# The quantised feed-forward of a two-layer decoder as one unrolled stream in place of four loops

## What is computed

```python
def act_qdq(x):
    qmax = 2.0 ** (ACT_BITS - 1) - 1.0
    scale = jnp.maximum(jnp.max(jnp.abs(x)) / qmax, 1e-12)
    return jnp.clip(jnp.round(x / scale), -qmax - 1.0, qmax) * scale

x = act_qdq(x)
up = act_qdq(x @ lpbq_dequant(w_up).T)
gate = act_qdq(x @ lpbq_dequant(w_gate).T)
sig = fixed_qdq_u16(jax.nn.sigmoid(gate))
gate = act_qdq(gate * sig)
o = act_qdq(gate * up)
return o @ lpbq_dequant(w_down).T
```

## Time and profile before

| | |
|---|---|
| three runs, us | 1874.87, 1876.58, 1877.08 |
| the profiled execution, us | 1876.91 |
| its span, first to last instruction, us | 1875.3 |
| mean granted clock of TensorE | 0.92 of full |
| busy: TensorE / DVE / ACT / POOL | 83% / 53% / 46% / 23% of the span |
| DMA traffic | 107 MB, 57 GB/s over the span |

### The profile page before, as it was taken

The page is one execution under the profiler, slowest core; times in us unless marked ns, Lnnn a source line. Parts: engine busy times, 40 slices in busy tenths (PEclk is TensorE's granted clock), DMA queues, the critical chain, the costliest instruction groups (busy, mean ns, idle before and its releaser), DMA issues. The chain is left out here.

```text
span 1875.3 us, 27409 instructions
## 1 busy us (share of the span) xinstructions
PE 1555.1 (83%) x10044; PEld 1078.4 (58%) x10044; DVE 986.9 (53%) x2215; ACT 871.9 (46%) x1820; POOL 435.4 (23%) x563
## 2 busy tenths in 40 slices
PE   4999999999875499999959999999996699740189
PEld 2666766676653287877736666666665343310177
DVE  3565657766655252222135565656453336888822
ACT  2346565555453122121126565556663337877611
POOL 3123233434333200000056444543331000000000
PEclk9999999999987699999979999999997799875599
DMA  3340111101311434343431111110000000000112
GB/s 103 125 150 19 42 32 45 39 30 42 105 35 49 144 104 149 109 144 120 116 107 42 31 43 33 50 38 1 16 15 23 0 0 1 0 0 0 46 66 68
DMA packets 99630, 107.08 MB, mean 57 GB/s; under 512 B 25266, under 2 KB 88508, under 8 KB 99504
## 3 DMA queue, kind: packets, MB, share of 16 engines
q1 hardware_dynamic: 93360, 88.83, 15.2%
q0 software_dynamic: 6144, 16.57, 2.7%
HBM read 63.59 MB, written 42.01 MB: 56 GB/s over the span
## 5 line engine op out<-in xcount | busy, mean ns | idle before, releaser
L1866 ACT ACTIVATE c_pr<-bank,c_nmax 128x256 f32<-128x256 f32 x256 | 118.1, 475 | 151.0 <-DVE c_nmax L1947 150.9
L2417 PE MATMUL bank<-wdT,hT_all 128*128 128x256 f32 x384 | 89.1, 397 | 119.5 <-DVE hT_all L2395 119.5
L1619 POOL TENSOR_SCALAR c_pr<-c_pr,c_rsum 128x256 f32<-128x256 f32 x256 | 128.7, 518 | 223.1 <-DVE c_rsum L1952 223.0
L1386 ACT ACTIVATE b_G<-bank 128x320 f32<-128x320 f32 x128 | 56.0, 437 | 209.5 <-PE bank L1336 209.5
L1336 PE MATMUL bank<-b_XT,shared 128*128 128x320 f32 x512 | 153.3, 434 | 0.0
L2417 PEld LDWEIGHTS bank<-wdT,hT_all 128*128 128x128 f32 x384 | 76.8, 201 | 132.2 <-DVE hT_all L2395 120.7
L1350 PE MATMUL bank<-shared,b_G 128*128 128x256 f32 x640 | 142.2, 379 | 0.0
L1350 PEld LDWEIGHTS bank<-shared,b_G 128*128 128x128 f32 x640 | 120.9, 190 | 17.8
L947 DVE TENSOR_TENSOR a_A<-bank,a_causal 128x512 f32<-128x512 f32 x128 | 79.4, 683 | 73.8 <-PE bank L475 73.7
L1947 DVE TENSOR_REDUCE c_nmax<-bank 128x2 f32<-128x512 f32 x128 | 82.2, 683 | 55.0 <-PE bank L1658 54.9
L1336 PEld LDWEIGHTS bank<-b_XT,shared 128*128 128x128 f32 x512 | 91.7, 191 | 27.0 <-issue 0.2
(11 more groups left out here) (287 smaller groups left out, 3403.5 us busy)
## 6 DMA issues: line engine op xcount, KB each, us to landing
shared<-L_ffn_w SPq DMA_DIRECT2D x32, 512.0 KB, 6.0
t_slots_in<-a_h SPq DMA_DIRECT2D x20, 512.0 KB, 6.7
shared<-t_slots_in SPq DMA_DIRECT2D x15, 640.0 KB, 6.9
t_slots_out<-b_Y SPq DMA_DIRECT2D x15, 640.0 KB, 4.1
a_xin<-x SPq DMA_DIRECT2D x8, 512.0 KB, 3.7
a_xr<-x SPq DMA_DIRECT2D x8, 512.0 KB, 3.7
t_x_a<-hT_all SPq DMA_DIRECT2D x8, 512.0 KB, 2.9
shared<-t_x_a SPq DMA_DIRECT2D x8, 512.0 KB, 4.1
```

Of the source, the lines that this page charges most:

```text
L1386: a.activation(G[e % 2][:, f, HC * m:HC * m + HC], P[2 + n % 2][:, 0:HC], ACT.Gelu).then_inc(q.g_ready, 1)
L1619: p.tensor_scalar(pr[k][:, e, u, :], pr[k][:, e, u, :], rsum[k][:, e, u:u + 1], 1.0, ALU.mult, ALU.mult).then_inc(q.pr_ready, 1)
L1866: a.activation(pr[t % 2][:, e, u, :], P[e][:, S * u:S * u + S], ACT.Exp, bias=nmax[t % 2][:, e, u:u + 1], accum_out=sums[t % 2][:, e, u:u ...
L2417: t = p.matmul(P[n % 8][:, 0:D], tl[f"of{k % 2}"][:, f, 128 * j:128 * j + 128], wdT[:, f, :], start=(f == 0), stop=(f == FC - 1))
```

## The change

The feed-forward becomes one block with one set of semaphores: no loop, no block end or clear between its stages.

- At the end of layer 1 POOL runs one `partition_all_reduce` on a scratch column, whose result is not used.
- Input: DVE alone quantises, a group (2 x 512 elements) at a time: groups 0 and 1 ahead of the gate, the others between the gate's magnitudes.
- Gate: 48 units in one run; TensorE goes on with the up units as soon as a bank is free.
- Activation: tiles are now two units (2 x 512 = 1024 elements in each partition), 24 of them. The multiplied activation is written over the gate in `raw` and kept. There is one sigmoid tile (`sig`), two for its uint16 values and three for the gate's int16; every third tile is rounded by ACT, the others by DVE.
- Up values: 13 tiles have room of their own (`up`); 7 go into columns of `hT_all` whose products are done; 4 tiles (8 units) stay in the 8 PSUM banks until they are converted. Units 46 and 47 take the banks of units 42 and 43.
- Product: ACT converts the up value and the kept activation to int16; DVE multiplies and takes the magnitude.
- Down: the rows of x are fetched once the first 8 up tiles are converted, into their room; 8 groups in one run with two int16 tiles; the last group is stored in four parts of 128 KB.

```diff
+                p.partition_all_reduce(rstd[0][:, 0:1], minus[:, 0:1], 128, RMAX).then_inc(q.c_pool, 1)
...
-        make_scales(("x", c.amax, None, None))
-        quantise_input()
...
-            with nc.Fori(0, NG // K) as i:
...
+        IN_BANKS = (19, 20, 22, 23)
+        def unit_bank(m):
+            return P[m % 8] if m < NU - 2 else P[m % 8 - 4]
+        def up_tile(n):
+            if n < NOWN:
+                return pair(up[:, W * n:W * n + W])
+            i = n - NOWN if n < 19 else NG - 2
+            return hT[:, :, T * i:T * i + T]
+        def sig_by_scalar(n):
+            return n % 3 == 2
...
+            @block.sync
+            def _(s):
+                s.wait_ge(q.ui_ready, NG * NT * D // W)
+                for g in range(NG):
+                    s.dma_start(xin[g], x_rows[g]).then_inc(arrived[g], 16)
...
+            @block.tensor
...
+                for m in range(NU):
+                    if m % FC == 0:
+                        p.wait_ge(q.xq_ready, m // FC + 1)
+                    if m >= 8:
+                        p.wait_ge(q.bank_free, m - 7)
+                    product(wgT, m, P[m % 8])
+                for m in range(NU):
+                    p.wait_ge(q.bank_free, NU + m - (7 if m < NU - 2 else 3))
+                    product(wuT, m, unit_bank(m))
...
+            @block.scalar
...
+                def gate_int(n):
+                    if n >= 3:
+                        a.wait_ge(q.act_ready, n - 2)
+                    a.activation(pair(gi[n % 3]), tile(n), ACT.Copy, scale=inv["g"][:, :]).then_inc(q.gi_ready, 1)
+                def sigmoid(n):
+                    if n:
+                        wait_sig_int(a, n - 1)
+                    a.wait_ge(q.gi_ready, n + 1)
+                    a.activation(sig, gi[n % 3], ACT.Sigmoid, scale=scale["g"][:, :]).then_inc(q.sig_ready, 1)
+                def sigmoid_int(n):
+                    a.wait_ge(q.sig_ready, n + 1)
+                    a.wait_ge(q.act_ready, n - 1)
+                    a.activation(sq[n % 2], sig, ACT.Copy, scale=65536.0).then_inc(q.sq_ready_s, 1)
...
+                for m in range(4):
+                    keep_up(m)
+                a.wait_ge(q.scaled, 2)
+                gate_int(0)
+                gate_int(1)
+                sigmoid(0)
+                for n in range(1, NTILE):
+                    if n + 1 < NTILE:
+                        keep_up(2 * n + 2)
+                    sigmoid(n)
+                    if n + 1 < NTILE:
+                        gate_int(n + 1)
+                    if sig_by_scalar(n):
+                        sigmoid_int(n)
+                    if n + 1 < NTILE:
+                        keep_up(2 * n + 3)
+                a.wait_ge(q.scaled, 3)
+                for n in range(NTILE):
+                    if n >= NI:
+                        a.wait_ge(q.prod_ready, n - NI + 1)
...
+                        x = a.activation(pair(u_room[n % NI]), up_tile(n), ACT.Copy, scale=inv["u"][:, :])
+                    x.then_inc(q.ui_ready, 1)
+                    if n:
+                        if n == 1:
+                            a.wait_ge(q.scaled, 4)
+                        a.activation(pair(a_room[n % NI]), tile(n), ACT.Copy, scale=inv["a"][:, :]).then_inc(q.ai_ready, 1)
...
+            @block.vector
...
+                make_scale("x", 0)
+                quantise_input(0)
+                quantise_input(1)
+                for m in range(NU):
+                    gate_magnitude(m)
+                    if m % FC == 1 and m // FC + 2 < NG:
+                        quantise_input(m // FC + 2)
+                v.wait_ge(q.bank_free, NU)
+                largest("g")
+                make_scale("g", 1)
+                for m in range(4):
+                    up_magnitude(m)
+                sigmoid_int(0)
+                for n in range(NTILE):
+                    if n + 1 < NTILE and not sig_by_scalar(n + 1):
+                        sigmoid_int(n + 1)
+                    activate(n)
+                    if n + 2 < NTILE:
+                        up_magnitude(2 * n + 4)
+                    if n + 1 < NTILE:
+                        act_magnitude(n)
+                    if n + 2 < NTILE:
+                        up_magnitude(2 * n + 5)
...
+                largest("u")
+                act_magnitude(NTILE - 1)
...
+                make_scale("u", 2)
+                make_scale("a", 3, (scale["g"][:, :], 1.0 / 65536.0))
+                v.tensor_scalar(pair(a_room[0]), tile(0), inv["a"][:, :], None, ALU.mult).then_inc(q.ai_first, 1)
+                for n in range(NTILE):
+                    product(n)
+                    if n:
+                        product_magnitude(n - 1)
+                product_magnitude(NTILE - 1)
```

More of the change, by code:

```diff
@@ L2107, in feed_forward @@
         P = c.banks
-        ident = c.ident[:, :]
         NTOK = B * S
-        wuT, wgT, wdT = c.wuT, c.wgT, c.wdT
+        NU = NG * FC
+        NTILE = NU // 2
+        W = 2 * T
+        wuT, wgT, wdT, hT = c.wuT, c.wgT, c.wdT, c.hT_all
         raw = sb("raw", [128, FC, NTOK])
[L2112 to L2117, removed]
@@ L2118, in feed_forward @@
-        scale = {k: sb("scale_" + k, [128, 1]) for k in "xugao"}
-        inv = {k: sb("inv_" + k, [128, 1]) for k in "xugao"}
-        unit = {k: sb("unit_" + k, [128, 1]) for k in "ao"}
[L2123 to L2147, removed]
-                            if unit is not None:
-                                step(v.tensor_scalar(gmx[n][:, :], gmx[n][:, :], unit[:, :], None, ALU.mult))
-                            step(v.tensor_scalar(scale[k][:, :], gmx[n][:, :], 1.0 / QMAX, 1e-12, ALU.mult, ALU.max))
-                            step(v.reciprocal(inv[k][:, :], scale[k][:, :]))
-                            if unit is not None:
-                                step(v.tensor_scalar(inv[k][:, :], inv[k][:, :], unit[:, :], None, ALU.mult))
-                        for m in zeroed:
-                            v.memset(m[:, :], 0.0)
-                clear(nc, q)
@@ L2158, in quantise_input @@
-        def quantise_input():
-            with ExitStack() as once:
-                q = signals(nc, once, "xi_ready xq_ready")
-                xi = raw[:, 0:1, :].bitcast(I16)
-                with nc.Block() as block:
-                    @block.scalar
-                    def _(a):
-                        part = xi[:, 0, 0:NTOK]
-                        a.activation(part, c.hT_all[:, 0, :], ACT.Copy, scale=inv["x"][:, :]).then_inc(q.xi_ready, 1)
-                        a.wait_ge(q.xi_ready, 1)
-                        a.activation(c.hT_all[:, 0, :], part, ACT.Copy, scale=scale["x"][:, :])
-                    @block.vector
-                    def _(v):
-                        part = xi[:, 0, NTOK:2 * NTOK]
-                        v.tensor_scalar(part, c.hT_all[:, 1, :], inv["x"][:, :], None, ALU.mult).then_inc(q.xq_ready, 1)
-                        v.wait_ge(q.xq_ready, 1)
-                        v.tensor_scalar(c.hT_all[:, 1, :], part, scale["x"][:, :], None, ALU.mult)
-                clear(nc, q)
@@ new lines, in unit_bank, with tile, kept_until @@
+        def unit_bank(m):
[5 more added lines that the diff above has]
+            return hT[:, :, T * i:T * i + T]
+        def tile(n):
+            f = n % (FC // 2)
+            g = n // (FC // 2)
+            return raw[:, 2 * f:2 * f + 2, T * g:T * g + T]
+        def kept_until(m):
+            return NU + sum(k // 2 not in IN_BANKS for k in range(m + 1))
@@ L2423 @@
+        clear(nc, q)
 class Common:
```

373 lines of the change are left out of this document (169 added, 204 removed).

## The result

| | before | after |
|---|---|---|
| median, us | 1876.83 (4 runs: 1874.87 to 1883.19) | 1807.47 (4 runs: 1804.15 to 1812.24) |
| ratio, 95% interval | | 0.9627 [0.9595, 0.9659] |
| profiled execution / its span, us | 1876.91 / 1875.3 | 1812.24 / 1810.5 |
| a second series on another chip, median, us | 1876.28 (9 runs) | 1804.69 (5 runs), ratio 0.9613 [0.9592, 0.9635] |

The change saves 69 to 72 us of a forecast 77.6. The profiled execution is the slowest of the nine of the changed kernel, so positions in it are told from a mark inside the layers that both kernels share: R, the start of POOL's last reciprocal root of layer 1, at 1444.98 before and 1456.92 after. From R to the span's end it was 430.3 us before and 353.6 after, 76.7 less. The rest of the miss lies ahead of R, in code that is the same.

The account below looks back on a forecast made before the run. Bounds: TensorE in gate and down, DVE in product, three engines almost level in up. Stage ends added in sequence to span 1797.6, time 1799.2, 1799 at the median, 77.6 us (4.1%) less; range 1789 to 1825.

Parts of the forecast that it names:

- The layer's end: Layer 1's end: early reduction takes the 6.8 us first-use gap; input maximum there at 1454.8, not 1458.6.
- the early reduction does nothing: Layer end: first-use cost can't begin before other work is done; real reduction 5.4 us later, 1804; chance 0.12.
- Input by groups: Input quantisation: TensorE starts at 1457.1, not 1468.17; the other seven groups, 1.3 us each on DVE, cost nothing.
- Gate: Gate stage: 48 units without a loop turn, 44.08 us with cold start plus 41.2; TensorE ends at 1542.4.
- Head of the up stage: From gate scale at 1545.2 through copies, gate integers, one table load and sigmoids to the first activation at 1557.0.
- The swap rival: Up stage: Copy and Sigmoid swap tables at each tile, 57 us more, 1856; chance 0.04.
- Activation and up: Up stage after the first activation: DVE bounds closely, 87.8 us, 3.65 a tile; last magnitude at 1645.0.
- hand-offs cost full durations: Two DVE-bound stages: each wait breaks the 0.09 us overlap, 153 operations, 14 us, 1813; chance 0.16.
- TensorE cools: Up stage: waiting drops TensorE to the lower clock, 77 us more, 1876, no gain; chance 0.03.
- The slower rival: Up stage: the single sigmoid tile serialises ACT and DVE, 83 us more, 1882; chance 0.03.
- Product: Product stage: DVE's 24 multiplies and 24 magnitudes take 54.2 us, ACT hidden at 2.12 against 2.26 a tile.
- Down: Down stage: one cold start in place of two, 86.2 us, 1707.4 to 1793.6; last store put at 3.6.

Follow-up runs that it names:

- experiment with the whole input: Changed kernel with all eight input groups quantised on DVE before the first gate unit; first gate matmul 26.18 us after R, +10.17.
- a pass put back: Changed kernel with DVE instead of ACT converting the kept activation to int16 in the product stage; 1824.15 us, a to o reductions 71.90 for 57.06.
- the kernel with loads at the layer's start: Changed kernel with the early reduction moved from the end to the start of layer 1's POOL stream; 1830.47 us, R at 1473.61.
- the kernel before with one turn per loop: Kernel before with each of its four loops run as one turn of twice the length; 1841.42 us for 1879.31.

## Why the forecast was near, and where it failed

- **The layer's end: the step that failed.** "It is a cost of the first use. Moved to 1446.0 it ends at 1452.8" took one idle stretch for one cost. There were two, a 5.3 us drain of POOL under the other engines' last work and a 5.7 us load after it, and moving the load only put the drain behind it. In the clock of before the maximum was due at 1454.8 and came at 1458.97, 4.2 late. That is the outcome of the rival "the early reduction does nothing", which had 0.12 and was priced at 5.4. Its mechanism was not that of the trace: the load did start early. A row of non-busy instructions of POOL would have told it in advance; the view of busy instructions cannot.
- **Input by groups** held: 2.4 us from the reduction to the first gate matmul, for 9.9 before, and the other six groups for nothing (experiment with the whole input: +10.17 when they stand ahead).
- **Gate**: 84.3 us for 85.3. The one cold start cost 1.9 us (84.3 less 48 units of 1.716), not the 2.9 of the earlier trace rows's first turn. It varies: from first matmul to the g reduction the eleven executions of this stage fall into 86.0 to 86.3 and 87.1 to 87.4.
- **Head of the up stage**: first activation at 1560.0 in the clock of before, for 1557.0; 2.6 of the 3.0 were already there at the gate's scale. The one table load was there (1.28 us, and 1.32 from the end of the gate integer to the sigmoid's start), and no second one. The swap rival (0.04) is out.
- **Activation and up**: 89.4 us for 88.0 (87.8 and the largest's 0.2). Of the 1.4 us, 1.1 is a slip of the sum: it counts 23 magnitudes of the activation up to the last one, and the program has 24 (x24 in the row below). The pitch of instructions in a row held, so "hand-offs cost full durations" (0.16) is out: it asked for up to 9.5 us more here. "TensorE cools" (0.03) is out, at 0.94 of clock; it did cool before the last two units (5.60 us for their eight matmuls), hidden as forecast. The slower rival, one sigmoid tile that serialises ACT and DVE (0.03), is out: ACT waited for conversions 11.4 us in all, but DVE waited for sigmoids only in the head (3.8 and 1.2 us) and from the first activation on not at all, busy 99.9% of the time. The groups that show it:

```profile
L2258 ACT ACTIVATE wgT<-d_gate_int,d_scale_g 128x1024 f32<-128x1024 int16 x24 | 27.5, 1148 | 11.4 <-DVE wgT L2355 6.2 <-DVE d_sig_int L2355 5.2
...
L2364 DVE TENSOR_REDUCE d_cur_a<-d_raw 128x1 f32<-128x1024 f32 x24 | 29.1, 1213 | 0.0
```
```profile
1646.72 5.60 PE L2217 MATMUL bank<-hT_all,wuT 128*128 128x512 f32 x8 [7.87 <-DVE d_cur_u L2349]
```

- **Scales**: 1.6 us for 2.4 (u and a) and 1.6 for 2.2 (o). **Product**: 54.6 for 54.2. ACT's 2.12 us a tile stayed under DVE's 2.26. The count of the passes that are left was right, and a pass put back measured +14.8.
- **Down**: 84.6 us for 86.2, one cold start again cheaper than counted; the last store's end 2.7 us after the last addition for 3.6 (a 128 KB part lands 1.7 us after its issue, at the median).
- So behind R the sum was 352.6 and came out 353.6. Lost were 3.9 us up to the first gate matmul and some 2.3 in the head of the up stage, the stage and the product; won back were 1.0 in the gate, 1.6 in the scales, 1.6 in down and 0.9 in the last store. That it came so near is in part luck of signs.
- **Ahead of R: the other step that failed, one not written down.** The sum took the layers in front for fixed. In twelve executions of kernels with the same code there, R lies between 1444.98 and 1459.73 us: 14.7 us apart (the kernel with loads at the layer's start left out). Two executions of the changed kernel itself have 1456.92 and 1446.5, 10.4 us apart, which is nearly all of 1810.5 to 1800.1 in their spans. One place where it arises, in the windows of the three (before, after, after again):

```profile
434.00:436.00 2.00, 2.00 (x3) 0.35 (x2) 0.45 (x2) 0.00 (x0) 1.40 (x2) 0.55 0.27 98
436.00:438.00 2.00, 1.11 (x25) 0.76 (x24) 0.00 (x0) 1.76 (x4) 1.51 (x2) 1.00 0.28 98
```
```profile
436.00:438.00 2.00, 0.96 (x5) 0.34 (x8) 0.00 (x0) 1.32 (x3) 1.70 (x2) 0.50 0.37 131
442.00:444.00 2.00, 2.00 (x15) 1.54 (x15) 0.36 (x1) 0.84 (x2) 1.55 (x1) 0.50 0.00 0
446.00:448.00 2.00, 2.00 (x21) 1.84 (x19) 0.00 (x0) 1.69 (x4) 0.00 (x0) 1.00 0.04 8
```
```profile
432.00:434.00 2.00, 1.14 (x3) 0.66 (x4) 1.90 (x8) 0.00 (x0) 1.70 (x2) 1.00 0.38 135
434.00:436.00 2.00, 1.11 (x10) 0.31 (x13) 0.65 (x3) 1.12 (x3) 1.39 (x3) 1.00 0.18 66
```

  All three have the same lull of TensorE before 433 us (2.9 us). Before, it is granted 2.4 GHz again at 436 us; in the repeat it isn't taken down at all; in the profiled execution of after it is granted 2.4 GHz only near 446, and the next step of DVE comes at 449.26 us, for 445.10 before and 443.75 in the repeat. Further steps of 1 to 2 us follow, near 500 us and from 980 us on; how much of them is the clock was not worked out. The Trainium skill ("TensorE: Matmul & The Clock Gate", The HAM clock gate) says that the cold stretch at a start varies from run to run with the phase of the gate, and that the penalty is under 1% of a typical span. The first the rows bear out. The second no run here measures by itself; the whole spread of 14.7 us is 0.8% of the span.
- **Open.** The nine executions of the changed kernel have a median of 1804.7, which puts R near 1449.4 with 353.6 behind it and 1.75 around the span; that of before (1876.6) puts it at 1444.7 by the same sum. Whether these 4.7 us are chance or something in the changed program, no run here settles. A part of R goes with the chip or the series: the three executions of the first chip that bear on it have 1459.3 to 1459.7, and the kernel before was slowest there too (1885.43). Nor is it tried what POOL's 5.3 us drain waits for.

## What to carry to other kernels

Count a loop's turns before its instructions: nearly half of this gain was to be had with four turns fewer. Most of the rest (33 of the other 41 us) came in the product stage, where DVE passes are left out: against the kernel before with one turn per loop DVE is busy 26 us less there. Before moving a cost to where it seems free, list what else ends an engine's block, its non-busy instructions included: what stood under other engines' work may be next in line. And where a stage is full, predict it by its bounding engine's passes at their pitch in a row: 54.2 against 54.6 us, and 14.8 us for a pass put back.

## What the runs showed of the chip that was not expected

- POOL's drain at the end of a block took 5.3 us in the two blocks in which POOL issues indirect DMAs (layer 0 as well: the row below), 34 to 38 ns in the feed-forward's blocks in which POOL has no work, and 0.07 us beyond the reduction in those that hold one. Its length is steady: 5.28 to 5.29 us for the first block and 5.31 for the second in all thirteen executions. That the indirect DMAs are its cause is a guess: in before the last of their transfers had landed at 1262 us, 183 us ahead of the second block's drain, and both blocks also hold POOL's arithmetic.

```profile
L303 POOLq DRAIN  x1: 5284/5284/5284, 634.0 to 634.0; - x1
```

- POOL's reciprocal root and its reduction over partitions displace each other's library. A swap to the reduction costs 5.6 to 5.9 us, the one swap back to the root was 8.5 us from the configuration instruction to the root; both show as idle time without a releaser.
- A table load on ACT took 1.28 us, and one ahead of the gate, for which nobody waited, served all later sigmoids.
- The same program's executions differ by up to 14.8 us (1870.64 to 1885.43 over fifteen runs of the kernel before, on several chips; by 10.5 over nine on one). One step of 4.2 us between two executions was traced to the granted clock.
